# Causal attention in two passes on one core: other PSUM banks for the second pass, and another order of the matrix work

## What is computed

```python
sim = jnp.einsum('bhid,bhjd->bhij', q, k) / math.sqrt(hd)
sim = jnp.where(causal, neg, sim)
p0 = jax.nn.softmax(sim); entropy = jnp.sum(-p0 * jnp.log(p0 + 1e-09), axis=-1, keepdims=True)
beta = jnp.where(entropy > 0.5, jnp.maximum(poly(entropy), 1.0), 1.0)
out = jnp.einsum('bhij,bhjd->bhid', jax.nn.softmax(sim * beta), v)
return out.transpose(0, 2, 1, 3).reshape(b, n, d) @ Wo.T + bo
```

## Time and profile before

| what | value |
|---|---|
| median of the runs shown | 2247.43 us (2245.31 to 2250.18) |
| profiled execution, its own time | 2242.66 us |
| its span | 2240.9 us, clock 0.769 |
| PE busy | 1603.5 us (72%) |
| DVE busy | 1481.3 us (66%) |
| ACT busy | 1393.9 us (62%) |

### The profile page before, as it was taken

The page is one execution under the profiler, slowest core; times in us unless marked ns, Lnnn a source line. Parts: engine busy times, 40 slices in busy tenths (PEclk is TensorE's granted clock), DMA queues, the critical chain, the costliest instruction groups (busy, mean ns, idle before and its releaser), DMA issues. The chain is left out here.

```text
span 2240.9 us, 22322 instructions
## 1 busy us (share of the span) xinstructions
PE 1603.5 (72%) x6402; PEld 675.5 (30%) x6402; DVE 1481.3 (66%) x3478; ACT 1393.9 (62%) x2635; POOL 142.2 (6%) x126
## 2 busy tenths in 40 slices
PE   4787899999999544677776777677776777511166
PEld 2343344444444101222223322232222222201144
DVE  6655444545453899877788777887778763379922
ACT  4564443434333697899988999889998976300012
POOL 0000000000000100000000000000000000035365
PEclk9998899999999655766768666676666778755578
DMA  4000165454556101101011010110101002240031
GB/s 146 0 1 0 37 156 155 132 154 129 154 152 164 49 34 46 64 23 61 32 37 60 27 62 27 37 61 31 61 25 40 33 31 79 58 122 0 0 101 50
DMA packets 56667, 147.36 MB, mean 66 GB/s; under 512 B 7760, under 2 KB 22480, under 8 KB 53936
## 3 DMA queue, kind: packets, MB, share of 16 engines
q1 hardware_dynamic: 52320, 136.63, 20.3%
q0 software_dynamic: 3072, 8.39, 1.2%
q10 hardware_dynamic: 1152, 0.92, 0.3%
HBM read 126.38 MB, written 19.53 MB: 65 GB/s over the span
## 5 line engine op out<-in xcount | busy, mean ns | idle before, releaser
L1668 DVE CUSTOM_DVE_ANT_0 sa_lg<-sa_e,sa_lg 128x1024 f32<-128x1024 f32 (+7 forms) x512 | 387.2, 756 | 162.9 <-ACT sa_lg L1559 162.7
L1411 PE MATMUL sa_ps<-sa_space 72*128 72x512 bf16 (+3 forms) x768 | 292.2, 449 | 223.0 <-DVE sa_nmax L1659 203.5
L1549 ACT ACTIVATE sa_e<-sa_e,sa_nmax 128x1024 f32<-128x1024 f32 (+7 forms) x512 | 406.0, 793 | 13.9 <-DVE sa_nmax L1659 13.5
L1567 ACT ACTIVATE sa_p<-sa_ps 128x512 f32<-128x512 f32 x576 | 342.5, 611 | 104.6 <-PE sa_ps L1458 53.4
L1559 ACT ACTIVATE sa_lg<-sa_e,sa_sum 128x1024 f32<-128x1024 f32 (+7 forms) x512 | 405.4, 792 | 2.7 <-DVE sa_prod L1668 2.2
L1659 DVE CUSTOM_DVE_ANT_0 sa_e<-sa_ps,sa_mask 128x1024 f32<-128x1024 f32 (+7 forms) x512 | 385.5, 753 | 16.8 <-PE sa_ps L1411 15.1
L1458 PE MATMUL sa_ps<-sa_q2s,sa_k2s 75*128 75x512 bf16 (+3 forms) x768 | 298.0, 425 | 89.4 <-ACT sa_p L1567 81.7
L974 DVE TENSOR_TENSOR mx_hw<-mx_spread,mx_h 128x512 f32<-128x512 f32 x256 | 176.1, 691 | 233.3 <-PE mx_ps L813 192.0
L875 ACT ACTIVATE mx_h<-mx_ps 128x512 f32<-128x512 f32 (+1 forms) x264 | 157.0, 597 | 277.7 <-PE mx_ps L800 257.2
L800 PE MATMUL mx_ps<-mx_f,m 128*128 128x512 f32 x512 | 261.4, 596 | 0.8 <-ACT mx_h L875 0.8
L813 PE MATMUL mx_ps<-mx_hw,m 128*128 128x512 f32 x512 | 259.8, 594 | 1.9 <-DVE mx_hw L974 1.9
(11 more groups left out here) (322 smaller groups left out, 1814.9 us busy)
## 6 DMA issues: line engine op xcount, KB each, us to landing
mx_spread<-mx_spill SPq DMA_DIRECT2D x256, 256.0 KB, 4.0
sa_space<-sa_spill_q SPq DMA_DIRECT2D x96, 96.0 KB
sa_space<-sa_spill_k SPq DMA_DIRECT2D x96, 96.0 KB
sa_k2s<-sa_spill_k SPq DMA_DIRECT2D x48, 192.0 KB
sa_q2s<-sa_spill_q SPq DMA_DIRECT2D x48, 192.0 KB
m<-m_in SPq DMA_DIRECT2D x1, 4256.0 KB, 18.4
records<-sa_e SPq DMA_DIRECT2D x8, 512.0 KB, 5.8
be_w<-w_in SPq DMA_DIRECT2D x16, 256.0 KB, 11.9
```

Source lines behind the costliest of these rows:

```text
L1411: last = nc.tensor.matmul(out[:, col:col + w], q_ring[:, c % 2, local, i * P:(i + 1) * P], k_ring[:, c % 2, local, col:col + w], start=Tru ...
L1549: nc.scalar.activation(e[:, u % 5, 0:w], e[:, u % 5, 0:w], ACT.Exp, scale=-1.0, bias=nmax[:, b % 2, i, h:h + 1], accum_out=sums[:, b % 2, ...
L1567: nc.scalar.activation(p_t[:, v % 2, hh, :], ps[:, 4 + m % 2, :], ACT.Exp, scale=-1.0).then_inc(exp2_ready.sem, 1)
L1668: nc.vector.tensor_tensor_reduce(out=lg[:, u % 2, 0:w], in0=e[:, u % 5, 0:w], in1=lg[:, u % 2, 0:w], scale=1.0, scalar=0.0, op0=ALU.mult, ...
```

## The change

It makes three things different, and leaves all arithmetic as it is.

First, the banks. Wide units and all preparation and finishing blocks take banks 0 and 1 (`both`); narrow units take bank 2 (`low`). Each waits for the last user of the same place (`before`, `holder`). The pieces take banks 3, 4 and 5 in a ring, and bank 2 joins the ring at the first piece of position 512 (`late`), when no unit is left.

Second, PE's order: at a position the pieces (with their answer) come right behind the unit, and the blocks behind the pieces.

Third, positions: widen 6 to 7, shift 8 to 9, q 86 to 87, k 88 to 89, values 106 to 107, the turn of the answers 8 to 9, attended 12 to 13, projection 16 to 17, and the expert scores of the first three batches from ALL1 + 14 to ALL1 + 17. So every block that DVE or ACT reads is now at an odd position, behind a narrow unit. DVE's readers move with them; the splits of the queries, the copy of the answers and SP's positions stay.

```diff
--- before.py
+++ after.py
@@ -1112,7 +1112,7 @@
 FIRST2 = SIDE_UNITS + 22
 GROUP_UNITS = UNITS1 // GROUPS
 AHEAD = 2
-SCORES_FROM, SCORES_STEP = ALL1 + 14, 24
+SCORES_FROM, SCORES_STEP = ALL1 + 17, 24
 LAST_SCORES = FIRST2 + ALL1 + 18
 END = LAST_SCORES + SCORES_STEP
 
@@ -1198,8 +1198,7 @@
         def tiles_of(v):
             return v.rearrange("p (t c) -> p t c", t=TILES)
 
-        slots = (flat(0), flat(2))
-        acc = flat(6)
+        both, low, acc = flat(0), ps[:, 2, :], flat(6)
 
         buffers = (sb("sa_sums", [P, TILES]), sb("sa_cent", [P, TILES, CH]), sb("sa_sq", [P, TILES, CH]),
                    sb("sa_var", [P, TILES]), sb("sa_log", [P, TILES]), sb("sa_rstd", [P, TILES]), eps)
@@ -1250,9 +1249,9 @@
         ident = mat(m1, MATS1, "ident")
         mask_q, mask_k = masks[:, 0:P], masks[:, P:2 * P]
 
-        WIDE_AT, SHIFT_AT = 6, 8
-        A_AT, Q_AT, K_AT, V_AT = 83, 86, 88, 106
-        TURN_AT, ATT_AT, PROJ_AT = 8, 12, 16
+        WIDE_AT, SHIFT_AT = 7, 9
+        A_AT, Q_AT, K_AT, V_AT = 83, 87, 89, 107
+        TURN_AT, ATT_AT, PROJ_AT = 9, 13, 17
 
         def slot_uses():
 
@@ -1266,14 +1265,28 @@
                          ("norm", scores_at(u, 15)), ("score", scores_at(u, 18)))
                 yield from ((what, n) for what, n in found if n is not None)
 
-        turn = {use: k for k, use in enumerate(slot_uses())}
-        users = {k: use for use, k in turn.items()}
+        def in_low(use):
+            return use[0] == "unit" and unit1(use[1])[2] < BANK // P
+
+        before, holder = {}, {}
+        for use in slot_uses():
+            before[use], holder[in_low(use)] = holder.get(in_low(use)), use
+
+        late = pieces2_at(ALL1).start
+        ring, bank_of, piece_before = [(3, None), (4, None), (5, None)], [], []
+        for m in range(GROUP * ALL2):
+            if m == late:
+                ring.insert(0, (2, None))
+            bank, user = ring.pop(0)
+            bank_of.append(bank)
+            piece_before.append(user)
+            ring.append((bank, m))
         freed = {"a": a_ready, "q": q_ready, "k": k_read, "v": v_ready, "shift": shift_ready, "wide": wide_read,
                  "unit": max_ready, "turn": att_ready, "att": att_copied, "proj": x_ready,
                  "norm": n_ready, "score": score_ready}
 
         def slot_of(what, n):
-            return slots[turn[what, n] % 2]
+            return low if in_low((what, n)) else both
 
         def centred_turn(b):
             return BATCH - 1 + 2 * b
@@ -1370,11 +1383,10 @@
             @block.tensor
             def _(pe):
                 def take_slot(what, n):
-                    k = turn[what, n]
-                    if k >= 2:
-                        last_user, m = users[k - 2]
-                        pe.wait_ge(freed[last_user].sem, m + 1)
-                    return slots[k % 2]
+                    if before[what, n] is not None:
+                        user, m = before[what, n]
+                        pe.wait_ge(freed[user].sem, m + 1)
+                    return slot_of(what, n)
 
                 def fill_a(b):
                     pe.wait_ge(ln.scaled.sem, b)
@@ -1450,9 +1462,11 @@
                     g, s = divmod(v, NPACKS)
                     if m % GROUP_PIECES == 0:
                         pe.wait_ge(stacked2[g % 2].sem, 16 * (2 * PARTS + 1) * (g // 2 + 1))
-                    if m >= 2:
-                        pe.wait_ge(exp2_ready.sem, m - 1)
-                    out, col = ps[:, 4 + m % 2, :], 0
+                    if m == late:
+                        pe.wait_ge(max_ready.sem, ALL1)
+                    elif piece_before[m] is not None:
+                        pe.wait_ge(exp2_ready.sem, piece_before[m] + 1)
+                    out, col = ps[:, bank_of[m], :], 0
                     for j, q, w in PACKS[s]:
                         own = q == j * P
                         last = nc.tensor.matmul(out[:, col:col + w], k2_ring[:, g % 2, hh, j * P:(j + 1) * P],
@@ -1510,6 +1524,10 @@
                 for u in range(END):
                     if u + AHEAD < ALL1:
                         score(u + AHEAD)
+                    for m in pieces2_at(u):
+                        second(m)
+                        if m % GROUP == GROUP - 1 and m >= GROUP:
+                            answer(m // GROUP - 1)
                     if (k := side_at(u, WIDE_AT)) is not None:
                         widen(k)
                     if (k := side_at(u, SHIFT_AT)) is not None:
@@ -1532,10 +1550,6 @@
                         turn_normed(b)
                     if (b := scores_at(u, 18)) is not None:
                         score_experts(b)
-                    for m in pieces2_at(u):
-                        second(m)
-                        if m % GROUP == GROUP - 1 and m >= GROUP:
-                            answer(m // GROUP - 1)
                     if group_at(u, 2) == ALL_GROUPS - 1:
                         answer(ALL2 - 1)
 
@@ -1564,7 +1578,7 @@
                     act.wait_ge(s2_mm.sem, m + 1)
                     if v >= 2:
                         act.wait_ge(pv_mm.sem, v - 1)
-                    nc.scalar.activation(p_t[:, v % 2, hh, :], ps[:, 4 + m % 2, :], ACT.Exp, scale=-1.0
+                    nc.scalar.activation(p_t[:, v % 2, hh, :], ps[:, bank_of[m], :], ACT.Exp, scale=-1.0
                                          ).then_inc(exp2_ready.sem, 1)
 
                 def log_sums(k):
```

## The result

| | before | after |
|---|---|---|
| median of 20 runs each | 2247.95 us (2240.25 to 2253.69) | 2254.15 us (2247.36 to 2259.24) |
| ratio | | 1.0027, 95% interval 1.0019 to 1.0036 |
| profiled execution: span, clock | 2240.9 us, 0.769 | 2248.3 us, 0.764 |

The account below looks back on a forecast made before the run. Beside the units ACT bounds, with DVE setting the pace at widen; at the end PE bounds, with gaps. The terms -3 + 4 + 12 + 10 - 11 + 2 give +14 us, 2261.4 us, range 2228 to 2279.

Parts of the forecast that it names:

- widen: Six places beside pieces: pieces first and widen one position later gain 0.5 us each, -3 us in all.
- the turns: Turn of the answers beside units: ACT loses 0.9 us, thirteen times, +12 us; 0 to 1.4 each.
- q and k: Batch blocks a, q, k: DVE goes without a unit; 1.3 us per batch, three times, +4 us.
- What can be won is only DVE's idle time: At widen: 1.33 us for widen and 1.46 for the next unit, about 3 us with waits for ACT.
- The bank ring doesn't help: At the turns: the third bank is free, but the piece is behind the waiting unit.
- Projection: Output projection: the reader delays ACT's piece by 1.2 to 1.9 us; 1.5, three times, +4.5 us.
- Attended rows and values: Turn of the attended rows and the values: ACT loses net 0.9 us, six times, +5.5 us.
- The end: The 78 us without units: four banks shorten the cycle of four pieces and an answer, -11 us; bounds 0 and 21.
- The chain to the last group: Last group's transfer through DRAM: last widen behind three pieces and an answer comes later, +2 us (0 to 4).
- A: Rival, faster: stalls at six widens and pieces go, DVE's slack carries the readers; 28 less, 2219 us; chance 0.14.
- B: Rival, about the same: PE nearly throughout at 2.4 GHz, all terms at fast ends; -5, 2242 us; chance 0.22.
- D: Rival: blocks' new waits and the end's gain cancel, turns 0.3 each, end 5 more; 2248 us; chance 0.12.

## Why the forecast was right in sign and too large

The readers' stalls came as the mechanism says, and the sum is too large because of two terms: widen, at -3 instead of -9.1 and -8.2, and the turns, at +12 instead of +7.7 and +8.0. That the sign came out right was in part luck: q and k were taken too low (+4, measured +6.0 and +8.0) and made up for some of it. With widen and the turns as measured the sum would have been +4 to +5 us, no more than two profiles of the changed kernel differ by beside the units.

**Widen: the term was mis-sized, and this is the largest error.** "What can be won is only DVE's idle time", taken at 0.5 us each; measured 1.4 to 1.5. That DVE's wait for widen counts held: doubling widen cost its length. Two things were wrong. One is the length. The forecast set 0.9 us of waiting if widen ran at 2.4 GHz and 2.7 if at 1.2, and went about midway; in two profiles seven of twelve ran in under 2.4 us. The other is that both bounds, 1.2 us gained and 0.8 lost, were about 1 us too low: places with the fastest widens won 2.07 to 2.16 us, and those at 3.15 to 3.19 still won 0.52 to 0.85. DVE in the changed kernel, where widen took 2.21:

```profile
1297.64 1.23 DVE L1720 TENSOR_TENSOR sa_q<-sa_ps,sa_q 64x1024 f32<-64x1024 f32 x1 [1.08 <-PE sa_ps L1431]
...
1299.52 1.09 DVE L1673 CUSTOM_DVE_ANT_0 sa_e<-sa_ps,sa_mask 128x896 f32<-128x896 f32 x1 [0.65 <-PE sa_ps L1423]
```

It waits 1.08 us for widen and 0.65 for the next unit, 1.73 us instead of 2.54 at the same place of the kernel before (1.33 and 1.21; 2.79 at the one of the earlier trace rows); the next unit was charged at 1.0. That is 0.8 us, and the place won 1.8. Most of the rest is what the forecast left out: DVE also waits less for ACT's logarithms in the units around widen, 2.9 us instead of 3.6 here. At the next place, where widen took 3.18 us, DVE waited 2.7 us for widen and the unit instead of 1.7, and for the logarithms 1.6 instead of 2.8, and 0.52 us were won all the same. "About 3 us with waits for ACT" was too small a sum to win from. At the second side, where no pieces run yet, ACT waits 4.27 us for the shift's block (2.33 before): the loss of 1.4 to 2.2 us that the forecast had not looked for.

**Turns: the mechanism is right, the size was 0.9, measured 0.64 to 0.67** (7.7 and 8.0 us over 12; the forecast counted 13 beside units, but the thirteenth has no unit behind it). Step by step at the turn shown, with T = 1125.70 (in both kernels the start of ACT's next instruction, while the row of the logarithm ends 0.15 us later): the reader ends at T + 1.74 (forecast 1.8), the unit starts 0.06 us later (forecast 0.29, read from a place where PE was not only waiting for the reader), the piece 0.39 later (0.39), ACT 0.42 later (0.5), and ACT wanted it at T + 2.38, not T + 2.22. That makes 0.23 at 2.4 GHz instead of 0.8; where PE ran at 1.2 GHz the stall was 0.82 (1.4). The sentence "The bank ring doesn't help" failed: the piece is indeed behind the unit, but without the third bank the block itself comes too late, and the turns cost 22.6 us. The sum took the block to be ready, which in this order of the work the third bank makes true. The pieces' new order counts too: with the blocks first the turns cost 16.2 us.

**Projection** 1.5 each, measured 0.8: same chain, same errors. **Attended rows and values** 5.5, measured 4.2 and 5.2: near in the sum only, and that is luck. All six were taken at 0.9; the attended rows cost 1.0 to 1.2 each, since they wait for PE's block too and not for the product alone, and the values 0.2 and 0.7. **a, q, k** 4, measured 6.0 and 8.0: too low. The changed kernel's k block runs 3.75 us at 1.2 GHz where in the kernel before part of it was faster (3.21 us in the same batch), and ACT waits 5.68 us for the piece behind it (3.20 before; changed kernel, timeline):

```profile
1189.74 3.75 PE L1403 MATMUL sa_ps<-sa_space,m 128*128 128x512 f32 x4 [0.41 <-DVE sa_nmax L1673]
...
1196.95 0.60 ACT L1581 ACTIVATE sa_p<-sa_ps 128x512 f32<-128x512 f32 x1 [5.68 <-PE sa_ps L1475]
```

Here the pieces' new place doesn't help, as they still are behind that block for the position after; that q and k bear more than DVE's reading was only seen, not tested apart.

**The end** -11, measured -13.2 and -12.1, and against the mean of both profiles of before (79.5, 75.0) -10.4. A cycle of four pieces and an answer takes 2.44 us at 2.4 GHz (forecast 2.3; before 2.98). Two answers of the changed kernel:

```profile
1849.79 1.04 PE L1491 MATMUL sa_ps<-sa_p,sa_space 128*9 128x512 f32 x8
...
1852.23 1.04 PE L1491 MATMUL sa_ps<-sa_p,sa_space 128*9 128x512 f32 x8
```

But it was all booked to the four banks, and 4 us are the order's. **The chain to the last group** +2, measured -1.7 and -1.9: the last widen took 1.96 us instead of 3.52, which outweighs its three pieces. The changed kernel with widen doubled shows it: there the last one took 3.71 us, and the chain 31.6 us instead of 29.9, as long as in the kernel before (31.6). PE waits longer for the transfer than in the earlier trace rows, as forecast, though the piece comes earlier; it has done its other work sooner:

```profile
1866.18 0.61 PE L1472 MATMUL sa_ps<-sa_q2s,sa_k2s 75*128 75x512 bf16 x1 [10.46 <-DMA sa_q2s<-sa_spill_s]
```

**The rivals.** A, that DVE's slack carries the readers, fell with the twelve waits for L1781. The rule beside it, of "Perfetto Trace Analysis" of the Trainium skill (Optimization Strategy), is that a gap that keeps repeating can mean too little SBUF or PSUM. The trace doesn't agree as to the six equal gaps that it was read from: with a ring of two banks the six places won 9.6 us, with three 9.1 and 8.2. It agrees at the turns of the changed kernel, which cost 22.6 us with two banks and 7.7 with three.

B, about the same, took all terms at their fast ends for a steadier clock. The clock from 890 to 1815 us stayed at 0.68, so beside the units its reason didn't come, though it rose from 0.83 to 0.90 in the end; and half of it is in the result, as widens and turns did run nearer their fast ends. The rule of "TensorE: Matmul & The Clock Gate" of the Trainium skill (A second HAM failure mode: psum-queue depth-cycling), that cycling through PSUM makes the clock swing, has no support in the means here. With the ring cut to two the clock of that stretch was 0.64 instead of 0.68, but the kernel before has a ring of two and 0.68 (0.67 in its second profile), and the changed kernel at the old places has a ring of three and 0.64.

D, a cancelling, is nearest to the measured sum of the first profile (+1.0). The median of 2254 us lies about midway between D's 2248 and the forecast's 2261. Of D's reasons a turn cost 0.64, between its 0.3 and the forecast's 0.9, and the end gave 1 to 2 us more, not 5. The upper end of the range has a slip: the forecast with thirteen turns at 1.4 and the end giving 5 less is 2273 us, not 2279.

## What to carry to other kernels

When a freed bank is to relieve a stall, ask what gives the bank up: in the changed kernel the ring's third bank was worth 16 to 21 us beside the units (1096.6 us with two, 1075.3 to 1080.5 with three), and what it took, the second pair for wide units with the positions that this needs, cost more than that (the kernel before has 1063.0 and 1063.6 with a ring of two). Taking more banks only where the units are over, moving widen by a position and putting the pieces ahead of it and of the blocks at the end made the kernel 0.9% faster instead of 0.3% slower. A block that the bounding engine waits for costs about its own length. On TensorE the same 16 matmuls took anything from 1.93 us, all at 2.4 GHz, to 3.68, all at 1.2: look in each version whether the engine stood still directly ahead of the block, and give the term both ends, as the same work ahead of it still left 1.96 and 3.18 us here. And where ACT was kept waiting, count also what the engine behind it waits for ACT. To size such terms, set the starts of one repeated instruction of both kernels against each other: the steps name the places.

## What was not expected of the hardware

Two profiles of one kernel can differ by 5.0 us (before: 747.4 and 752.4) and 5.8 us (changed: 753.2 and 747.3) ahead of any changed code, and by 5 us beside the units (1075.3, 1080.3 and 1080.5 for the same code). Over all profiles widen's 16 matmuls take from 1.93 to 3.68 us. A difference of 6 us in the run medians is therefore not to be read off one pair of profiles: the first pair shows 1.0 us of it inside the attention. And in one set of runs the part behind the attention took 267 us instead of 283, in all four kernels profiled there. Why is open: the record gives a later set the same chip number, 11, and there it took 283.
